# Second attention layer: the way of the turned probabilities from blocks to their places, through DRAM in place of inside SBUF

## The chip, the cores and the metric

The kernel runs on one core of one Trainium2 chip. The metric is the device time of one execution in microseconds (us), the median of several runs. The core's engines are TensorE (PE: matmuls), VectorE (DVE), ScalarE (ACT), GpSimd (POOL) and SyncE (SP). SP does no arithmetic here; it issues all transfers. Each transfer is then carried by the core's 16 DMA engines. SBUF is the on-chip memory of 128 partitions, PSUM the banks that TensorE writes, DRAM the memory outside.

## The reference, cut to what matters

Two layers, each an attention and a feed-forward, over a residual stream `x` of shape (2, 512, 512), all in float32. The change touches the second attention only:

```python
# x: (b=2, n=512, 512); H = 32 heads of HD = 128
h = layernorm(x)
q = rmsnorm((h @ Wq + bq).reshape(b, n, H, HD), gq)
k = rmsnorm((h @ Wk + bk).reshape(b, n, H, HD), gk)
v = (h @ Wv + bv).reshape(b, n, H, HD)
scores = einsum("bnhd,bmhd->bhnm", q, k) / sqrt(HD)
attn = softmax(scores, axis=-1)              # (2, 32, 512, 512)
out = einsum("bhnm,bmhd->bnhd", attn, v).reshape(b, n, H * HD)
x = x + layernorm(out @ Wo + bo)
x = x + layernorm(swiglu_ffn_with_lora(layernorm(x)))
```

## The kernel before

One function per stage runs in turn: the first attention (`grouped_attention`), a linear feed-forward, the second attention (`paired_attention`, from L660 on), then the feed-forward with the gate (`swiglu_phase`). Every fp32 product is made of three passes over a high and a low part of each operand (`product`, L83 to L85); the high part is a rounding copy by ACT, the low part a subtraction (`rest`, L90) by DVE or POOL.

**Groups, slots, tiles.** The second attention works in 8 groups of 4 heads (`NG` passes). A group has 8 slots, each one head of one of the two batches, and a slot has 4 tiles (`TB`) of 128 query rows by 512 keys. So there are 64 slots and 256 tiles. Every engine walks over the same 32 steps `n` of a group, one tile's scores per step, and at each step does what tables of numbers say is due. The tables `USES1`, `OUTS1`, `LOADS1` and `FETCH1` give the steps of the projections, the weights and the outputs; `TURN_AT, MOVE_AT, LAND_AT, PV_AT, REST_AT = 1, 4, 8, 10, 12` gives how many steps after a slot's first tile each of its parts comes. Nothing but semaphores ties the engines together, so one may be steps ahead of another. In the last group the steps run on past 32, and there the first pieces of the next stage (`Entry`) are mixed in.

**One slot.** TensorE makes a tile's scores. DVE takes the negated row maximum (L1052). ACT takes the exponential into `probs` and the row sum (L941). The product with v needs the probabilities with the keys on the partitions, so they must be transposed. DVE does this in blocks of 32 by 32 (L1067): a block is turned within its own 32 partitions and is put into `blocks`. After that, a block of query group `g` and key group `c` lies in partitions 32g to 32g+31, and its place is partitions 32c to 32c+31. The moving is done by transfers, from `blocks` to `moved`. Both tiles hold two slots, even and odd (`k = slot % 2`), of 8 KB per partition each.

**The step that is changed** is `move` on SP (L780 to L800), four steps after the slot's first tile. SP waits for the reciprocal row sums (L783) and for the last read of `inv_rows` (L785), and writes the sums to DRAM, turned, 512 elements of 4 bytes (L786). It waits for the four transposed tiles (L790) and for the product of the slot two before (L792). Then it issues 16 transfers of 32 partitions by 2 KB (L796), one per pair of g and c. Last, it reads the sums back as a broadcast into `inv_all` (L799). Each transfer raises a semaphore by 16 when it has landed; `s_move[k]` counts 16 x 16 = 256 (`MOVES`) per slot.

**Who waits.** Eight steps after the slot's first tile ACT waits for `s_move[k]` and makes the high parts `probsT_hi` (L947), two at that step and two at the next. POOL and DVE make the low parts `probsT_lo` (L90). At step 10 TensorE multiplies with v (`pv`, into `l_general`), DVE scales the result by `inv_all` (L1023), and ACT and DVE split it for the output projection (L959, L1078), whose results DVE adds to `acc` (L1085). Before DVE overwrites `blocks` it waits until the slot two before has been moved.

**What else SP has in its queue.** In order of the steps: the weights of q and k (L761, eight transfers, at steps 6 and 22), of v (L765, four, at steps 1 and 17, after a wait at L752 for TensorE to have finished with v's last projection), of the output (`raw_out`, L768, two, at steps 11 and 27, with a wait at L755), and biases (L774). In the last group there are also the residual rows and side weights of the next stage (L376, L380, at step 22), its weights (L384, L386, at step 26) and more rows (L376, at step 33). SP works through all this in order, so a wait holds up what follows.

```python
for g in range(TB):
    for c in range(TB):
        sp.dma_start(moved[32 * c:32 * c + 32, k, g],
                     blocks[32 * g:32 * g + 32, k, c]).then_inc(s_move[k], 16)
wait_past(sp, s_inv_dma, m, 32 * SLOTS, 32 * slot + 16)
sp.dma_start(inv_all[:, k], ...).then_inc(s_inv_dma, 16)
```

Of the kernel before, what the change touches and what calls it, by code (L numbers as in the profile page):

```python
# [20 lines left out]
F32 = mybir.dt.float32  # L21
F32R = mybir.dt.float32r

P = 128
B, S, D = 2, 512, 512
T = B * S
TT = T // P
TB = S // P
# [5 lines left out]
SLOTS = GH * B  # L34
# [25 lines left out]
def wait_past(engine, sem, m, per, count):  # L60

    if m.first and not (isinstance(count, int) and count > 0):
        return
    engine.wait_ge(sem, m.i * per + count)
# [176 lines left out]
class Opening:  # L241


    first, last, i = True, False, 0
# [18 lines left out]


MOVES = TB * TB * 16
TURN_AT, MOVE_AT, LAND_AT, PV_AT, REST_AT = 1, 4, 8, 10, 12


# [388 lines left out]
                self.square(act, 0, t)  # L657


def paired_attention(p, ctx0, xT, acc, ident, half, inv_rows, ahead, entry):  # L660

    nc, a = p.nc, p.a
    start = Opening()
    with ExitStack() as ctx:
# [18 lines left out]
        blocks = sb("blocks", [P, 2, TB, TB, P])  # L683
        with ExitStack() as early:
            moved = p.sb(early, "l1_moved", [P, 2, TB, TB, P])
# [57 lines left out]
        @block.sync  # L743
        def _(sp):
            def fetch(m, x, d):
                kind, r = x
                if not (m.first and d == 0 and r == 0) and m is not start:
                    was = d - (r == 0)
                    if kind == "wqk":
                        sp.wait_ge(s_bank, m.done(USES1, ("y", 1 - r, 0, 0), was))  # L750
                    elif kind == "wv":
                        sp.wait_ge(s_bank, m.done(USES1, ("v", 1 - r, 1, 1), was))  # L752
                    else:
                        sp.wait_ge(s_out, m.done(OUTS1, (1 - r, 1, TB - 1), was))
                    sp.nop(nofuse=True)  # L755
                group = m.i + d if m is not start else 0
                cols = slice(r * HW, (r + 1) * HW)
                if kind == "wqk":
                    for c in range(C):
                        for e in range(2):  # L760
                            sp.dma_start(raw_qk[:, r, c, e * HW:(e + 1) * HW],  # L761
                                         a[("l1_wq", "l1_wk")[e]][group * C + c][:, cols]).then_inc(s_raw[kind][r], 16)
                elif kind == "wv":
                    for c in range(C):
                        sp.dma_start(raw_v[:, c], a["l1_wv"][group * C + c][:, cols]).then_inc(s_raw[kind], 16)  # L765
                else:
                    for h in range(2):
                        sp.dma_start(raw_out[:, h], a["l1_wo"][group * GH + 2 * r + h]).then_inc(s_raw[kind], 16)  # L768

            def bias(m, r, d):  # L770
                group = m.i + d if m is not start else 0
                for e in range(2):
                    rows = a[("l1_bq", "l1_bk")[e]][bass.ds(group, 1)][:, r * HW:(r + 1) * HW]
                    sp.dma_start(b_qk[:, r, e * HW:(e + 1) * HW], rows.to_broadcast([P, HW])).then_inc(s_b[r], 16)  # L774

            sp.wait_ge(s_const, 32)
            sp.dma_start(b_v_all[:], a["l1_bv"]).then_inc(s_const, 16)
            sp.dma_start(acc[:, 0], a["l1_bo"].to_broadcast([P, D])).then_inc(s_const, 16)

            def move(m, slot):  # L780
                k = slot % 2
                wait_past(sp, s_inv, m, SLOTS, slot + 1)
                sp.nop(nofuse=True)  # L783
                wait_past(sp, s_inv_dma, m, 32 * SLOTS, 32 * slot)
                sp.nop(nofuse=True)  # L785
                sp.dma_start(inv_rows[k].rearrange("t p -> p t"), inv[:, TB * (slot % SLOTS):TB * (slot % SLOTS + 1)],  # L786
                             allow_slow_non_contiguous=True)\
                    .then_inc(s_inv_dma, 16)
                wait_past(sp, s_block, m, TILES, TB * (slot + 1))
                sp.nop(nofuse=True)  # L790
                if not (m.first and slot < 2):
                    sp.wait_ge(s_free, m.done(USES1, ("pv", (slot - 2) % SLOTS), -1 if slot < 2 else 0))  # L792
                    sp.nop(nofuse=True)
                for g in range(TB):
                    for c in range(TB):
                        sp.dma_start(moved[32 * c:32 * c + 32, k, g],  # L796
                                     blocks[32 * g:32 * g + 32, k, c]).then_inc(s_move[k], 16)
                wait_past(sp, s_inv_dma, m, 32 * SLOTS, 32 * slot + 16)
                sp.dma_start(inv_all[:, k], inv_rows[k].rearrange("t p -> (t p)").unsqueeze(0).to_broadcast([P, S]))\  # L799
                    .then_inc(s_inv_dma, 16)  # L800

            def body(m):
                for n in m.steps():
                    for x, d in m.turns(FETCH1, n):
                        fetch(m, x, d)
                    for x, d in m.turns(BIAS1, n):
                        bias(m, x[0], d)
                    slot = m.slot_at(n, MOVE_AT)
                    if slot is not None:
                        move(m, slot)  # L810
                    if m.last and n == Entry.ROWS_AT:
                        sp.wait_ge(s_free, m.done(USES1, ("y", 1, 1, TB - 1)))
                        entry.load_rows(sp, 0)
                        entry.load_side(sp)
                    if m.last and n == Entry.WEIGHTS_AT:
                        sp.wait_ge(s_free, m.done(USES1, ("tk", SLOTS - 1)))
                        entry.load_weights(sp)
                    if m.last and n == Entry.MORE_ROWS_AT:
                        entry.load_rows(sp, 1)

            passes(sp, body, Entry.END)

        @block.tensor
# [81 lines left out]
        def _(act):  # L905
# [37 lines left out]

            def landed_hi(m, slot, k):
                if k == 0:
                    wait_past(act, s_move[slot % 2], m, SLOTS // 2 * MOVES, (slot // 2 + 1) * MOVES)
                act.activation(probsT_hi[:, :, k], moved[:, slot % 2, :, k], ACT.Copy).then_inc(s_land_hi, 1)  # L947

            def output_hi(m, slot):
# [45 lines left out]
        def _(dve):  # L995
# [64 lines left out]
            def turn_blocks(m, n):  # L1060
                slot, t = divmod(n, TB)
                wait_past(dve, s_exp, m, TILES, n + 1)
                if t == 0 and not (m.first and slot < 2):
                    dve.nop(nofuse=True)
                    wait_past(dve, s_move[slot % 2], m, SLOTS // 2 * MOVES, slot // 2 * MOVES)
                to = blocks[:, slot % 2].rearrange("p c k x -> p k c x")[:, :, :, 32 * t:32 * t + 32]
                dve.transpose(to, probs[:, n % NPR]).then_inc(s_block, 1)  # L1067

# [1203 lines left out]
def build(nc, a, out):  # L2272
    p = Program(nc, a)
    with ExitStack() as ctx:
        ident = p.sb(ctx, "ident", [P, P])
        half = p.sb(ctx, "half", [P, TB * GH])
        acc = p.sb(ctx, "acc", [P, TT, D])
        xT, xT_words = p.split_and_words(ctx, "xT", [P, C, T])
        made = p.sem(ctx, "made")
        x_rows = a["x"].rearrange("(t p) d -> p t d", p=P)  # L2280
        out_rows = out.rearrange("(t p) d -> p t d", p=P)
        kept = nc.dram_tensor("x_kept", [T, D], F32, kind="Internal").ap().rearrange("(t p) d -> p t d", p=P)

        inv_rows = [nc.dram_tensor(f"inv_rows{layer}", [2, tiles, P], F32, kind="Internal").ap()
                    for layer, tiles in enumerate((2 * TB, TB))]

        with nc.Block() as block:
            @block.gpsimd
            def _(pool):
                pool.memset(ident[:], 0.0).then_inc(made, 1)  # L2290
                pool.wait_ge(made, 1)
                pool.affine_select(out=ident[:], in_=ident[:], compare_op=ALU.not_equal, fill=1.0, base=0,
                                   pattern=[[-1, P]], channel_multiplier=1).then_inc(made, 1)
                pool.memset(half[:], -0.5).then_inc(made, 1)
                pool.wait_ge(made, 3)

        ahead = Ahead(p, ctx, xT)
        entry = Entry(p, ctx, xT, acc, ident, half, kept)
        grouped_attention(p, ctx, xT, acc, ident, half, x_rows, kept, inv_rows[0], ahead)
        paired_attention(p, ctx, xT, acc, ident, half, inv_rows[1], ahead, entry)  # L2300
        swiglu_phase(p, ctx, xT, xT_words, acc, kept, out_rows, entry)


# [58 lines left out]
```

## Time and profile before

| what | value |
|---|---|
| median of 3 runs | 2200.83 us |
| lowest and highest run | 2198.38 and 2201.15 us |
| the profiled execution | 2198.5 us, span 2196.7 us |
| granted clock of TensorE, mean over the span | 0.984 |
| PE, DVE, ACT, POOL busy | 2089.8, 1636.8, 1348.5, 1222.3 us |
| bytes moved by DMA | 231.69 MB, mean 105 GB/s |
| second attention, from its first moves to its last product | about 854 to 1965 us |

Times within the profile are us from the start of the span. A row of the time line gives an instruction's start, its duration, its engine, its line and what it writes and reads (out<-in), then in brackets how long the engine had been idle before it and what ended this. For SP, a row is the issue of one or more transfers, not their duration. The DMA view has one digit per fortieth of its stretch, the busy share of the 16 DMA engines in tenths, with the GB/s below it; its list of issues gives KB per transfer and the median time from issue to landing, where landings could be assigned. A granted clock of 1.00 is the full level of 2.4 GHz.

### The profile page before, as it was taken

What the parts mean: (1) busy time and instruction counts of PE and PEld (TensorE: products, weight loads), DVE (VectorE), ACT (ScalarE), POOL (GpSimd) and SP (SyncE); (2) the same over time, 40 slices, a digit from 0 to 9 for tenths busy, and PEclk for the clock granted to TensorE, in tenths of its full rate; (3) what the DMA queues carried; (4) which work ended last, traced back from release to release, by engine and by line L of the source; (5) the groups of instructions that cost most, each with busy time, mean ns of one, the idle gap of its engine ahead of it and who ended that gap; (6) DMA issues with size and microseconds to landing.
All of it is one profiled execution on the core that took longest, in us unless ns stands there. A gap on an engine that the chain in (4) does not pass through costs nothing. (4 is left out here: it accounts for less than half of the span.)

```text
span 2196.7 us, 37916 instructions
## 1 busy us (share of the span) xinstructions
PE 2089.8 (95%) x10535; PEld 1757.2 (80%) x10535; DVE 1636.8 (75%) x2972; ACT 1348.5 (61%) x3637; POOL 1222.3 (56%) x985
## 2 busy tenths in 40 slices
PE   6999999999999879999999999999999999868998
PEld 4788888888888657888888888888888888756786
DVE  6778888888788776778777777777777787775422
ACT  5777777777776455656566565666656665544321
POOL 3878778787786554546454554545445463354300
PEclk9999999999999989999999999999999999979999
DMA  2644444434444513555454455444554444643210
GB/s 83 131 105 126 108 110 114 115 104 127 102 119 129 140 55 69 105 122 114 114 108 104 109 119 115 109 99 111 118 115 111 99 111 93 142 95 105 87 53 25
DMA packets 219135, 231.69 MB, mean 105 GB/s; under 512 B 100528, under 2 KB 130384, under 8 KB 218992
## 3 DMA queue, kind: packets, MB, share of 16 engines
q1 hardware_dynamic: 218992, 229.97, 43.7%
q8 instruction: 67, 1.10, 0.3%
q14 instruction: 76, 0.62, 0.2%
HBM read 114.23 MB, written 6.55 MB: 55 GB/s over the span
## 5 line engine op out<-in xcount | busy, mean ns | idle before, releaser
L90 POOL TENSOR_TENSOR l_probsT_lo<-l_moved,l_probsT_hi 128x512 fp32r<-128x512 f32 (+2 forms) x256 | 280.4, 1100 | 296.7 <-ACT l_probsT_hi L947 269.2
L941 ACT ACTIVATE l_probs<-l_score,l_negtop 128x512 f32<-128x512 f32 x256 | 175.8, 687 | 373.2 <-DVE l_negtop L1052 359.9
L90 DVE TENSOR_TENSOR l_probsT_lo<-l_moved,l_probsT_hi 128x512 fp32r<-128x512 f32 (+1 forms) x256 | 292.5, 1143 | 37.4 <-ACT l_probsT_hi L947 37.0
L1052 DVE TENSOR_REDUCE l_negtop<-l_score 128x1 f32<-128x512 f32 x256 | 175.7, 687 | 93.1 <-PE l_score L85 90.6
L1833 ACT ACTIVATE l_probs<-l_score,l_negtop 128x128 f32<-128x128 f32 (+3 forms) x256 | 134.7, 526 | 170.3 <-DVE l_negtop L1946 169.4
L83 PE MATMUL l_out<-l_w_out_lo,l_oT_hi 128*128 128x512 f32 x512 | 209.0, 408 | 6.2 <-DVE l_oT_lo L1078 4.0
L83 PE MATMUL l_score<-l_kT_lo,l_qT_hi 128*128 128x512 f32 (+3 forms) x512 | 191.0, 373 | 22.4 <-POOL l_qT_lo L90 8.9
L1946 DVE CUSTOM_DVE_ANT_0 l_score<-l_score,l_mask 128x128 f32<-128x128 f32 (+3 forms) x256 | 125.9, 492 | 106.9 <-PE l_score L85 105.5
L84 PE MATMUL l_out<-l_w_out_hi,l_oT_lo 128*128 128x512 f32 x512 | 201.7, 394 | 0.0
L85 PE MATMUL l_out<-l_w_out_hi,l_oT_hi 128*128 128x512 f32 x512 | 201.5, 393 | 0.0
L83 PE MATMUL l_general<-l_w_qk_lo,xT_hi 128*128 128x512 f32 x504 | 198.1, 393 | 2.5 <-PEq L1452 2.5
L84 PE MATMUL l_general<-l_w_qk_hi,xT_lo 128*128 128x512 f32 x504 | 198.1, 393 | 0.0
L85 PE MATMUL l_general<-l_w_qk_hi,xT_hi 128*128 128x512 f32 x504 | 197.4, 392 | 0.0
L83 PE MATMUL l_general<-l_probsT_lo,l_v_hi 128*128 128x512 f32 (+3 forms) x512 | 182.2, 356 | 14.4 <-POOL l_probsT_lo L90 9.2
L85 PE MATMUL l_general<-l_probsT_hi,l_v_hi 128*128 128x512 f32 (+3 forms) x512 | 184.9, 361 | 0.0
L84 PE MATMUL l_general<-l_probsT_hi,l_v_lo 128*128 128x512 f32 (+3 forms) x512 | 184.4, 360 | 0.0
L85 PE MATMUL l_score<-l_kT_hi,l_qT_hi 128*128 128x512 f32 (+3 forms) x512 | 184.1, 359 | 0.0
L84 PE MATMUL l_score<-l_kT_hi,l_qT_lo 128*128 128x512 f32 (+3 forms) x512 | 183.5, 358 | 0.0
L1067 DVE STREAM_TRANSPOSE l_blocks<-l_probs 128x512 f32<-128x512 f32 x256 | 177.8, 695 | 5.6 <-ACT l_probs L941 5.6
L90 POOL TENSOR_TENSOR l_w_qk_lo<-l_raw_qk,l_w_qk_hi 128x512 fp32r<-128x512 f32 x60 | 77.7, 1295 | 150.5 <-ACT l_w_qk_hi L915 150.5
L646 ACT ACTIVATE l_squares<-l_y 128x128 f32<-128x128 f32 x512 | 151.9, 300 | 11.2 <-DVE l_y L1010 11.2
L947 ACT ACTIVATE l_probsT_hi<-l_moved 128x512 fp32r<-128x512 f32 x256 | 146.9, 629 | 4.7 <-DMA l_moved<-l_blocks 4.7
(249 smaller groups left out, 6235.7 us busy)
## 6 DMA issues: line engine op xcount, KB each, us to landing
l_moved<-l_blocks SPq DMA_DIRECT2D x1024, 64.0 KB
l_moved<-l_blocks SPq DMA_DIRECT2D x512, 80.0 KB
l_inv_all<-inv_rows SPq DMA_DIRECT2D x32, 512.0 KB
l_raw_out<-l_wo SPq DMA_DIRECT2D x64, 256.0 KB, 4.3
l_inv_all<-inv_rows SPq DMA_DIRECT2D x64, 256.0 KB
l_raw_q<-l_wq SPq DMA_DIRECT2D x32, 256.0 KB, 4.0
l_raw_qk<-l_wq SPq DMA_DIRECT2D x64, 128.0 KB, 2.8
l_raw_qk<-l_wk SPq DMA_DIRECT2D x64, 128.0 KB, 2.9
```

The lines of the kernel that those rows point to most:

```text
L83: nc.tensor.matmul(out, left.hi, right.lo, start=first, stop=False, skip_group_check=True)
L84: nc.tensor.matmul(out, left.lo, right.hi, start=False, stop=False, skip_group_check=True)
L85: return nc.tensor.matmul(out, left.hi, right.hi, start=False, stop=last, skip_group_check=True)
L90: return engine.tensor_tensor(out, full, hi.bitcast(F32), ALU.subtract)
L646: last = act.activation(self.squares[:, h], self.y[:, b, t, h * HD:(h + 1) * HD], ACT.Square, accum_out=self.sumsq[:, b, j:j + 1])
L941: act.activation(probs[:, n % NPR], score[n % 2][:], ACT.Exp, bias=negtop[:, n:n + 1], accum_out=total[:, n:n + 1]).then_inc(s_exp, 1)
L947: act.activation(probsT_hi[:, :, k], moved[:, slot % 2, :, k], ACT.Copy).then_inc(s_land_hi, 1)
L1052: dve.tensor_reduce(negtop[:, n:n + 1], score[n % 2][:], AXX, ALU.max, negate=True)\
L1067: dve.transpose(to, probs[:, n % NPR]).then_inc(s_block, 1)
L1833: act.activation(probs[:, n % NPR, 0:width[t]], score[n % 2][:, 0:width[t]], ACT.Exp, bias=negtop[:, n:n + 1], scale=-1.0, accum_out=total ...
L1946: dve.tensor_tensor_reduce(out=score[n % 2][:, 0:w], in0=score[n % 2][:, 0:w], in1=mask[:, S - w:S], scale=-SCALE, scalar=3.0e38, op0=ALU. ...
```

## The change

A DRAM tensor `block_rows` is added, of two halves (even and odd slots) of 128 rows by 8 KB. `move` now ends with one store of all of a slot's `blocks` into its half, 1 MB. A new function `land`, one step later in the program, waits until this store has landed and issues four loads. Load c fills partitions 32c to 32c+31 of `moved` with the four query groups' blocks, 4 x 2 KB for each partition, 256 KB in all. The read of `inv_all` moves to the end of `land`. `s_move[k]` now counts (1 + 4) x 16 = 80 (`LANDS`) per slot, and the waits of ACT and DVE count accordingly.

```diff
+LANDS = (1 + TB) * 16
@@ move, on SP
-                for g in range(TB):
-                    for c in range(TB):
-                        sp.dma_start(moved[32 * c:32 * c + 32, k, g],
-                                     blocks[32 * g:32 * g + 32, k, c]).then_inc(s_move[k], 16)
+                sp.dma_start(block_rows[k], blocks[:, k].rearrange("p c t x -> p (c t x)")).then_inc(s_move[k], 16)
+
+            def land(m, slot):
+                k = slot % 2
+                wait_past(sp, s_move[k], m, SLOTS // 2 * LANDS, slot // 2 * LANDS + 16)
+                sp.nop(nofuse=True)
+                for c in range(TB):
+                    rows = block_rows[k].rearrange("(g i) (c x) -> c i g x", g=TB, c=TB)[c]
+                    sp.dma_start(moved[32 * c:32 * c + 32, k].rearrange("p g t x -> p g (t x)"), rows)\
+                        .then_inc(s_move[k], 16)
                 wait_past(sp, s_inv_dma, m, 32 * SLOTS, 32 * slot + 16)
                 sp.dma_start(inv_all[:, k], ...)
@@ body, on SP
                     if slot is not None:
                         move(m, slot)
+                    slot = m.slot_at(n, MOVE_AT + 1)
+                    if slot is not None:
+                        land(m, slot)
@@ landed_hi, on ACT
-                    wait_past(act, s_move[slot % 2], m, SLOTS // 2 * MOVES, (slot // 2 + 1) * MOVES)
+                    wait_past(act, s_move[slot % 2], m, SLOTS // 2 * LANDS, (slot // 2 + 1) * LANDS)
@@ turn_blocks, on DVE
-                    wait_past(dve, s_move[slot % 2], m, SLOTS // 2 * MOVES, slot // 2 * MOVES)
+                    wait_past(dve, s_move[slot % 2], m, SLOTS // 2 * LANDS, slot // 2 * LANDS)
@@ the launch
+        block_rows = nc.dram_tensor("block_rows", [2, P, TB * S], F32, kind="Internal").ap()
```

On TensorE, DVE, ACT and POOL the order of the instructions stays as it was. On SP it changes in each slot. At the layer's entry, the first slot, SP had:

```order
L765 DMA l_raw_v<-l_wv 128x256 x4
L786 DMA inv_rows<-l_inv 128x4x1
L796 DMA l_moved<-l_blocks 32x512 x16
L799 DMA l_inv_all<-inv_rows 128x512
L761 DMA l_raw_qk<-l_wq 128x256
```

and has now:

```order
L766 DMA l_raw_v<-l_wv 128x256 x4
L787 DMA inv_rows<-l_inv 128x4x1
L795 DMA block_rows<-l_blocks 128x2048
L803 DMA l_moved<-block_rows 32x4x512 x4
L806 DMA l_inv_all<-inv_rows 128x512
L762 DMA l_raw_qk<-l_wq 128x256
```

The 16 moves became one store and four loads, in the same place. At the layer's end, slots 59 to 61 of the last group, SP had:

```order
L796 DMA l_moved<-l_blocks 32x512 x16
L799 DMA l_inv_all<-inv_rows 128x512
L765 DMA l_raw_v<-l_wv 128x256 x4
L786 DMA inv_rows<-l_inv 128x4x1
L796 DMA l_moved<-l_blocks 32x512 x16
L799 DMA l_inv_all<-inv_rows 128x512
L376 DMA ffn_w_near_words<-x_kept 128x4x512
L380 DMA ffn_w_near_words<-f_a 96x512 x2
L380 DMA ffn_w_near_words<-f_b 96x512
```

and has now:

```order
L795 DMA block_rows<-l_blocks 128x2048
L766 DMA l_raw_v<-l_wv 128x256 x4
L803 DMA l_moved<-block_rows 32x4x512 x4
L806 DMA l_inv_all<-inv_rows 128x512
L787 DMA inv_rows<-l_inv 128x4x1
L795 DMA block_rows<-l_blocks 128x2048
L803 DMA l_moved<-block_rows 32x4x512 x4
L806 DMA l_inv_all<-inv_rows 128x512
L377 DMA ffn_w_near_words<-x_kept 128x4x512
L381 DMA ffn_w_near_words<-f_a 96x512 x2
L381 DMA ffn_w_near_words<-f_b 96x512
```

In every fourth slot the four transfers of v's weights come to stand between the store and the loads; all others keep their place behind `inv_all`.

## Rows read from the trace of the kernel before

**Rows 1.** The page's part 1, busy us and share of the span.

```profile
PE 2089.8 (95%) x10535; PEld 1757.2 (80%) x10535; DVE 1636.8 (75%) x2972; ACT 1348.5 (61%) x3637; POOL 1222.3 (56%) x985
```

**Rows 2.** Busy time by stretch; columns: stretch, length, PE, PEld, DVE, ACT, POOL, clock, DMA.

```profile
895.00:1886.00 991.00, 991.00 (x5243) 846.14 (x5242) 784.29 (x1183) 616.63 (x1918) 505.66 (x368) 1.00 0.50 109
```

**Rows 3.** Time line of SP, a quiet slot and the start of the next.

```profile
1405.45 0.38 SPq L786 DMA_DIRECT2D inv_rows<-l_inv  x1
1406.12 10.01 SPq L796 DMA_DIRECT2D l_moved<-l_blocks  x16
...
1422.71 10.02 SPq L796 DMA_DIRECT2D l_moved<-l_blocks  x16
```

**Rows 4.** Time lines of SP and ACT, slots 0 and 1.

```profile
853.76 12.24 SPq L796 DMA_DIRECT2D l_moved<-l_blocks  x16
...
871.91 10.02 SPq L796 DMA_DIRECT2D l_moved<-l_blocks  x16
...
867.49 1.15 ACT L947 ACTIVATE l_probsT_hi<-l_moved 128x512 fp32r<-128x512 f32 x2 [0.28 <-DMA l_moved<-l_blocks]
...
884.57 1.15 ACT L947 ACTIVATE l_probsT_hi<-l_moved 128x512 fp32r<-128x512 f32 x2 [1.56 <-DMA l_moved<-l_blocks]
```

**Rows 5.** Time line of ACT, the readings of the slots in rows 3.

```profile
1421.12 1.15 ACT L947 ACTIVATE l_probsT_hi<-l_moved 128x512 fp32r<-128x512 f32 x2
...
1440.78 1.14 ACT L947 ACTIVATE l_probsT_hi<-l_moved 128x512 fp32r<-128x512 f32 x2
```

**Rows 6.** Time lines of SP and ACT, a late slot in the steady stretch.

```profile
1649.97 15.65 SPq L796 DMA_DIRECT2D l_moved<-l_blocks  x16
...
1667.11 1.16 ACT L947 ACTIVATE l_probsT_hi<-l_moved 128x512 fp32r<-128x512 f32 x2 [1.39 <-DMA l_moved<-l_blocks]
```

**Rows 7.** Loads of 256 KB: SP's time line, then the issues' landings.

```profile
2092.41 1.75 SPq L2121 DMA_DIRECT2D xT_hi_words<-x_kept  x4
...
xT_hi_words<-x_kept SPq DMA_DIRECT2D x4, 256.0 KB, 3.2
xT_lo_words<-x_kept SPq DMA_DIRECT2D x4, 256.0 KB, 4.3
```

**Rows 8.** DMA view of 1897 to 1925 us, landings of the next stage's loads.

```profile
ffn_w_near_words<-x_kept SPq DMA_DIRECT2D x1, 1024.0 KB, 7.3
...
ffn_w_near_words<-f_b SPq DMA_DIRECT2D x1, 192.0 KB, 11.8
```

**Rows 9.** DMA view of 779 to 789 us, a store of 1 MB.

```profile
x_kept<-l_rope SPq DMA_DIRECT2D x1, 1024.0 KB, 4.4
```

**Rows 10.** DMA view of 1411 to 1412.5 us.

```profile
GB/s 0 0 328 109 164 273 164 382 109 109 55 55 0 0 0 0 0 0 0 109 109 219 55 0 0 109 0 0 109 0 0 55 0 0 0 55 55 55 109 55
...
q1 hardware_dynamic: 69, 0.11, 104.2%
```

**Rows 11.** Time line of SP, slots 61 and 62.

```profile
1902.67 0.50 SPq L380 DMA_DIRECT2D ffn_w_near_words<-f_b  x1
...
1905.63 10.30 SPq L796 DMA_DIRECT2D l_moved<-l_blocks  x16
...
1916.73 0.34 SPq L384 DMA_DIRECT2D ffn_tile_raw<-f_tile  x1
...
1920.72 1.01 SPq L768 DMA_DIRECT2D l_raw_out<-l_wo  x2
...
1922.51 12.21 SPq L796 DMA_DIRECT2D l_moved<-l_blocks  x16
```

**Rows 12.** Time line of ACT at the layer's end.

```profile
1934.02 0.63 ACT L915 ACTIVATE l_w_out_hi<-l_raw_out 128x512 fp32r<-128x512 f32 x1 [7.97 <-DMA l_raw_out<-l_wo]
...
1937.78 1.14 ACT L947 ACTIVATE l_probsT_hi<-l_moved 128x512 fp32r<-128x512 f32 x2
...
1956.77 2.17 ACT L947 ACTIVATE l_probsT_hi<-l_moved 128x512 fp32r<-128x512 f32 x4
```

**Rows 13.** Time line of DVE, the same place.

```profile
1938.95 1.35 DVE L90 TENSOR_TENSOR l_probsT_lo<-l_moved,l_probsT_hi 128x512 fp32r<-128x512 f32 x1 [0.17 <-ACT l_probsT_hi L947]
```

More of the change, by code:

```diff
@@ L657, in scalar, with paired_attention @@
                 self.square(act, 0, t)
-def paired_attention(p, ctx0, xT, acc, ident, half, inv_rows, ahead, entry):
+def paired_attention(p, ctx0, xT, acc, ident, half, inv_rows, block_rows, ahead, entry):
     nc, a = p.nc, p.a
@@ L2299, in build @@
         grouped_attention(p, ctx, xT, acc, ident, half, x_rows, kept, inv_rows[0], ahead)
-        paired_attention(p, ctx, xT, acc, ident, half, inv_rows[1], ahead, entry)
+        paired_attention(p, ctx, xT, acc, ident, half, inv_rows[1], block_rows, ahead, entry)
         swiglu_phase(p, ctx, xT, xT_words, acc, kept, out_rows, entry)
```

## The prediction

> **What bounds the kernel now.** I read the page's busy times first, then the busy times by stretch, then the queue of SP (the engine that only issues the transfers), then who waits for the moved probabilities. TensorE is busy 95% of the span [rows 1]. From 895 to 1886 us, nearly the whole second attention, it is busy 991.00 of 991.00 us at a granted clock of 1.00 [rows 2]. In that stretch nothing can be gained. Time can only be lost, and only if the moved probabilities come so late that TensorE runs dry. What is left is the entry of the layer (before 895 us) and its end (after 1886 us), where each engine waits for another.
>
> **The path of one slot.** In a quiet slot SP issues the transfer to `inv_rows` at 1405.45, the 16 moves from 1406.12 on (10.01 us, 0.63 us each) [rows 3]. How long the last move takes to land is seen where ACT waits for it: in slot 0 the moves run from 853.76 to 866.00, and ACT, idle for them, starts at 867.49, 1.5 us later [rows 4]. So a quiet slot takes 10.0 + 1.5 = **11.5 us** from its first move. ACT comes to read it at 1421.12, which is **15.0 us** after the first move; the next slot, first move 1422.71, is read at 1440.78, 18.1 us after [rows 3, 5]. So there are some 3.5 us to spare in the slots of the tighter kind. How much more is free is shown by one late slot: its moves took 15.65 us from 1649.97, ACT waited 1.39 us and read at 1667.11, 17.1 us after the first move, and TensorE lost nothing [rows 2, 6]. A slot may thus take 17 us, and I take 18 as the point at which TensorE starts to lose.
>
> **The change, part by part.** Per slot and on SP, 16 issues go and 5 come: one store of 1 MB to `block_rows`, and four loads of 256 KB back. A wait for the store stands between them. There are 64 slots. No other engine issues anything else or in another order, so all of the price is in when the probabilities land, and in what SP has queued behind its new wait.
>
> - *Issues.* An issue costs 1.75/4 = 0.44 us for this kind of load [rows 7]. The five cost 2.2 us instead of 10.0. As SP is off the bound in the steady stretch, this is worth nothing there.
> - *Loads.* Four loads of 256 KB from DRAM: issued at 2092.41, 1.75 us for four, landing in 3.2 us, and 4.3 us for the next four [rows 7]. The last starts 1.3 us after the first, so they take 1.3 + 4.3 = 5.6 us. Bounds: 1.3 + 3.2 = 4.5 below, and 7.3 above, a load of 1 MB beside other work [rows 8].
> - *Store.* Alone, a store of 1 MB from SBUF to DRAM lands in 4.4 us [rows 9]. That is the lower bound. The upper one is 11.8 us, the slowest landing that the views show in busy queues [rows 8]. Here the store follows `inv_rows`, 512 elements of 4 bytes written to DRAM. 5.5 to 7 us after the issue at 1405.45 the DMA engines stall: from 1411.0 to 1412.5 they are 104% busy over 69 packets, and in 18 of the 40 slices of that stretch nothing is moved [rows 10]. I read this as the small writes reaching memory only then, and the engines held up by them. Now the moves' issues hide it, since they last to 1416. A store issued at 1406.1 has all its data behind these writes. If it completes about when the stall ends, at 1412.5 plus 1 us, it takes **7.5 us**, and I take that value, between the bounds, since these rows come from the very place where the store will stand.
> - *Sum.* 7.5 + 0.1 for SP to go on + 5.6 = **13.2 us** against 11.5. With the bounds: 4.4 + 0.1 + 4.5 = 9.0 to 11.8 + 0.1 + 7.3 = 19.2.
>
> The Trainium skill (DMA: Bandwidth & Descriptors, section on queues, rings and completion order) says that a transfer's semaphore increment is a strongly ordered write, which lands only after every earlier write of that DMA engine, whatever its queue. By that rule the store can't be reported before the 4-byte writes are done, however short its own data are; without it the store would cost 4.4 us. No view here shows when `inv_rows` itself lands, but the stall agrees with the rule.
>
> - *Steady stretch (slots 3 to 58).* 13.2 is below 15.0 and far below 18: **0**. The cover is TensorE's own work and ACT's idle time before each exponential. In every fourth slot SP's four `wv` transfers now stand between store and loads, with their wait for TensorE (L752); those slots are of the roomy kind, and both fit in the 7.5 us in which SP waits anyway.
> - *Entry.* Slot 0: 13.7 us before, 13.2 after: 0. Slot 1: first move 871.91, ACT idle 1.56 us for it and reading at 884.57, 12.7 us after [rows 4]. Behind the eight weight transfers of 128 KB that SP issues before it (L761) the new path gives at least 13.2, and ACT and then TensorE move back by 0.5 to 1.5 us. I take **+1.0**.
> - *End.* Slot 61's first move is issued at 1905.63. Ahead of it are the residual rows, 1 MB, and side weights, of which the last, issued at 1902.67, lands 11.8 us later, 1914.5 [rows 8, 11]. The store ends no sooner. SP is then held till 1914.6, issues loads and `inv_all` (2.4 us) and comes to the weights of the feed-forward (L384, L386) at 1917.0, where it stood at 1916.73 [rows 11]; with some time for the store's own data behind all this, I take +1. `raw_out`, issued at 1920.72, kept ACT idle for 7.97 us until 1934.02, 13.3 us after its issue [rows 11, 12]. Slot 62's store is issued 1 us later than its first move was at 1922.51 [rows 11], at 1923.5, right behind `raw_out`. I give it the same 13.3 us, the nearest row, so 1936.8; with 0.1 + 5.6 its loads land at 1942.5. ACT read this slot at 1937.78 [rows 12]. It is now **4.7 us** late. DVE had been idle for it for 0.17 us [rows 13], and in DVE's order the residual sums (L1085) and the norm statistics of the next stage (L133) stand behind it. TensorE waits for the norms. So I count all 4.7. Slot 63 is read at 1956.77, 19 us after slot 62 and so with more room than in the steady stretch [rows 12]; it isn't late.
>
> Together +1.0 + 4.7 = **+5.7 us**, against the profiled execution of 2198.5 us: 2204.2. The median of the three runs shown is 2200.8, 2.3 above that execution, so the median after would be **2206.5 us**. What a measurement of this kernel can tell from no change is about 0.2%, 4.4 us: below 2196.4 is faster, above 2205.2 slower.
>
> **The rivals.**
>
> *Forecast, 0.48.* 2203 to 2212, by the value of the store in the full queues: three quarters of this is over the 0.2%.
>
> *Hidden at the end, 0.24.* If slot 62's store takes 8.5 us instead of 13.3, it lands at about the old 1937.8, and only the +1.0 at the entry stays: 2201.8; between 2199 and 2205. For it: the weights ahead of it are issued by 1920.7 and much of that will have landed by 1923.5. Against it: `raw_out` in the same place took 13.3.
>
> *Faster, 0.15, the other side.* If the small writes don't hold the store, it takes 4.4 us and the slot 4.4 + 0.1 + 5.6 = 10.1 instead of 11.5. The entry gains 1.4 us (ACT waits 1.56 there). At the end SP is free for the weights 4.4 + 0.1 + 2.4 = 6.9 us after slot 61's start instead of 10.9, `raw_out` comes up to 4 us earlier and so does the read of slot 62, of which some 3.4 would show: 2200.8 - 4.8 = 2196. It decides at a store under 5.8 us, from where the slot is shorter than 11.5. For it: the quiet store in rows 9. Against it: that one had no 4-byte writes ahead, and the stall in rows 10. In the skill, the rules for kernel authors on the same page favour it: coalesce small transfers, since under 64 KB one pays mostly overhead. By its fit of 2.0 us plus bytes over 436e3, an estimate from that page and made for another issuing path, 1 MB would take 4.4 us.
>
> *Much slower, 0.13.* If a quiet slot's path exceeds 18 us, TensorE runs dry each time. A store at 11.8 and loads at 6.9 give 18.8; 0.8 us over in 56 slots is 45 us: 2246. A milder form, with only those slots late in which SP stalls for some 3 to 5 us (15.65 instead of 10.01 in rows 6), gives 5 to 15 us over the layer: 2207 to 2222.
>
> Faster by over 0.2%: most of the faster case, 0.14. Within 0.2%: the hidden case and a quarter of the forecast's, 0.34. Slower: the rest, 0.52. The range 2194 to 2217 leaves out the worst of the much slower case and the best tenth of the faster one.
>
> **What would show it.** In the profile of the changed kernel: the store's issue and the first load's issue 7 to 8.5 us apart in quiet slots (under 6 speaks for faster, over 10 for much slower); TensorE still 100% busy from about 896 to 1887; ACT's idle time for the moved data in slots 0 and 1 at 0 to 3 us; and before slot 62 a new wait of ACT of 3 to 5 us, with all that follows shifted by that. I am wrong if the stretch from 895 to 1886 gets longer, or if slot 62 is read at the old distance from slot 61.

## The result, and the profile after

The changed kernel takes **2441.12 us** (median of 4 runs, 2437.76 to 2449.16) against 2199.61 us for the kernel before on the same chip (4 runs). The ratio is 1.1107, 95% interval 1.1073 to 1.114. The forecast of 2206.5 us had the sign right and the size wrong by 235 us; the range ended at 2217. Its profiled execution took 2437.76 us, with a span of 2436.0.

The busy times of the page after, beside [rows 1]:

```profile
PE 2170.9 (89%) x10535; PEld 1789.2 (73%) x10535; DVE 1636.0 (67%) x2972; ACT 1353.8 (56%) x3637; POOL 1208.7 (50%) x985
...
HBM read 181.34 MB, written 73.66 MB: 105 GB/s over the span
```

TensorE does the same 10535 matmuls. It is busy 81 us longer and idle 158 us longer (265.1 against 106.9). The steady stretch, busy time by stretch as in [rows 2]:

```profile
900.00:1880.00 980.00, 872.62 (x4325) 716.89 (x4323) 640.71 (x969) 511.92 (x1585) 409.22 (x306) 0.96 0.85 142
```

It was busy all of this stretch before; now it runs dry in nearly every slot (107 us in all, 2.3 per slot). Its granted clock falls from 1.00 to 0.96, and its busy time per matmul rises from 0.189 to 0.202 us. The DMA engines are busy 85% of the time in place of 50%, though they move only 142 GB/s.

**Where the time lies.** The reads of the moved probabilities on ACT's time line after, slots 0, 1, 61, 62 and 63, as in [rows 4, 12]:

```profile
872.26 1.15 ACT L957 ACTIVATE l_probsT_hi<-l_moved 128x512 fp32r<-128x512 f32 x2 [7.25 <-DMA l_moved<-block_rows]
...
892.15 1.15 ACT L957 ACTIVATE l_probsT_hi<-l_moved 128x512 fp32r<-128x512 f32 x2 [3.88 <-DMA l_moved<-block_rows]
...
2147.44 1.15 ACT L957 ACTIVATE l_probsT_hi<-l_moved 128x512 fp32r<-128x512 f32 x2 [4.61 <-DMA l_moved<-block_rows]
...
2172.30 1.15 ACT L957 ACTIVATE l_probsT_hi<-l_moved 128x512 fp32r<-128x512 f32 x2 [10.77 <-DMA l_moved<-block_rows]
...
2193.26 2.19 ACT L957 ACTIVATE l_probsT_hi<-l_moved 128x512 fp32r<-128x512 f32 x4 [1.80 <-DMA l_moved<-block_rows]
```

Before, slot 61 was read here:

```profile
1921.08 1.14 ACT L947 ACTIVATE l_probsT_hi<-l_moved 128x512 fp32r<-128x512 f32 x2
```

With slots 1, 62 and 63 of before at 884.57, 1937.78 and 1956.77 [rows 4, 12], the 239.3 us of span divide up as follows: up to slot 1 +7.6, slots 1 to 61 +218.8 (60 slots, 20.92 us each in place of 17.28), slot 61 to 62 +8.2, slot 62 to 63 +2.0, all after that +2.8.

**What SP does in a slot.** SP's time line after, two slots, beside [rows 3]:

```profile
1395.09 0.38 SPq L787 DMA_DIRECT2D inv_rows<-l_inv  x1
1395.74 0.37 SPq L795 DMA_DIRECT2D block_rows<-l_blocks  x1
1407.42 1.74 SPq L803 DMA_DIRECT2D l_moved<-block_rows  x4
1409.29 0.36 SPq L806 DMA_DIRECT2D l_inv_all<-inv_rows  x1
1415.79 0.38 SPq L787 DMA_DIRECT2D inv_rows<-l_inv  x1
1416.45 0.33 SPq L795 DMA_DIRECT2D block_rows<-l_blocks  x1
```

And what SP waits for in the layer, its waits from 900 to 2050 us (columns: engine and line, releaser, us in total, times, longest):

```profile
SPq L800 <- DMA block_rows<-l_blocks: 560.0, 55, 12.3
SPq L786 <- DMA l_inv_all<-inv_rows: 206.9, 54, 6.8
SPq L784 <- DVE l_inv L1068: 35.5, 22, 8.9
```

Two things are to be seen. The first load comes 11.68 us after the store; over slots 3 to 57 the median is 11.85. ACT reads this slot at 1415.16 after 4.09 us of idleness for it, 7.74 us after the first load. So the path is 11.68 + 7.74 = 19.4 us, where 11.5 stood before and 13.2 was forecast. And SP goes in a circle without rest: 0.65 us from `inv_rows` to the store, 11.68 to the loads, 1.87 to `inv_all`, then 6.50 until `inv_all` has landed, since the next slot's `inv_rows` waits for that (L786, at L785 before). Together 20.70 us, and TensorE's work in a slot is 17.3.

The DMA view of 1395 to 1408 us shows why the store is slow (digits: busy tenths, GB/s below):

```profile
DMA  9857599999900700000092969993323079710000
GB/s 372 315 192 52 184 403 429 353 88 25 25 0 0 25 0 0 0 0 0 0 50 25 126 50 101 50 126 25 50 50 50 25 328 403 303 51 0 0 0 0
```

A slice is 0.325 us. Up to 1398 data moves at up to 429 GB/s. Then, for some 7 us, little arrives (at most 126 GB/s in a slice, mostly 50 or less), until some 0.35 MB go in about a microsecond from 1405.4 on. I read this as the stall of [rows 10], now in front of somebody who waits.

### The profile page after: what moved, and what is told of

It reads as the page before. It is cut to its first block and busy times, and to the rows that moved or that the text cites. A ratio compares the mean times of both kernels' runs of the same rounds, so it can differ in the third digit from the quotient of the medians.

```text
span 2436.0 us, 37306 instructions
## 1 busy us (share of the span) xinstructions
PE 2170.9 (89%) x10535; PEld 1789.2 (73%) x10535; DVE 1636.0 (67%) x2972; ACT 1353.8 (56%) x3637; POOL 1208.7 (50%) x985
## 5 line engine op out<-in xcount | busy, mean ns | idle before, releaser
L83 PE MATMUL l_general<-l_probsT_lo,l_v_hi 128*128 128x512 f32 (+3 forms) x512 | 212.3, 415 | 169.8 <-DVE l_v_lo L90 106.7
L83 PEld LDWEIGHTS l_general<-l_probsT_lo,l_v_hi 128*128 128x128 f32 x512 | 108.8, 213 | 225.0 <-DVE l_v_lo L90 119.3
L84 PE MATMUL l_general<-l_probsT_hi,l_v_lo 128*128 128x512 f32 (+3 forms) x512 | 203.9, 398 | 0.0
L85 PE MATMUL l_general<-l_probsT_hi,l_v_hi 128*128 128x512 f32 (+3 forms) x512 | 203.8, 398 | 0.0
## 6 DMA issues: line engine op xcount, KB each, us to landing
block_rows<-l_blocks SPq DMA_DIRECT2D x64, 1024.0 KB, 11.9
```

The source lines that it names most:

```text
L83: nc.tensor.matmul(out, left.hi, right.lo, start=first, stop=False, skip_group_check=True)
L84: nc.tensor.matmul(out, left.lo, right.hi, start=False, stop=False, skip_group_check=True)
L85: return nc.tensor.matmul(out, left.hi, right.hi, start=False, stop=last, skip_group_check=True)
```

## The experiments

Two causes were on the table: W, the 512 small writes of `inv_rows` hold the store, and the circle on SP, where `inv_rows` waits for `inv_all`. Kernels 1 to 8 and 12 start from the changed kernel, 9 to 11 from the kernel before. "Period" below is the mean distance of the stores over slots 3 to 57 (20.92 us in the changed kernel), "store" the median landing in the DMA view or time line. Kernels 1 to 3, 5 to 7 and 12 were run once each; the differences of 70 us and more that are read from them are far above the spread of the kernel before, 2190 to 2204 us over all its runs.

**1. The store ahead of the small writes.**

```diff
+                sp.dma_start(block_rows[k], ...).then_inc(s_move[k], 16)
                 wait_past(sp, s_inv, ...); wait_past(sp, s_inv_dma, ...)
                 sp.dma_start(inv_rows[k].rearrange("t p -> p t"), ...)
-                sp.dma_start(block_rows[k], ...).then_inc(s_move[k], 16)
```

> The changed kernel with one step moved: SP issues the store of the blocks first and the transfer of the row sums to inv_rows (512 elements of 4 bytes) right behind it. In the changed kernel the store's median landing is 11.9 us and a slot takes about 21 us. Theory W (the small writes ahead of it hold the store up): the store lands in 4.5 to 6 us, the slot's period falls to the 17.4 us of the kernel before, and the time is 2195 to 2215 us. Rival S (the store is slow by itself: DRAM, or packets of 8 KB): it still takes about 12 us and the time stays above 2400 us.

Measured: 2290.80 us, period 18.57. It was expected near the time of before, so this is a miss. The stores still land in 11.9 us (median; single ones from 4.3 to 15.8). A slot of its time line:

```profile
1406.68 0.33 SPq L788 DMA_DIRECT2D block_rows<-l_blocks  x1
1408.98 0.38 SPq L793 DMA_DIRECT2D inv_rows<-l_inv  x1
1418.72 1.74 SPq L803 DMA_DIRECT2D l_moved<-block_rows  x4
```

The small writes were issued 2.3 us behind the store, and it is slow all the same. Over slots 3 to 57 they came 0.5 to 5.8 us behind (the expectation of kernel 5 says within a microsecond, which is true of 12 of these 55). How late they came matters: in the 10 slots with at most 0.75 us, 7 stores had landed after 4.4 to 5.9 us; in the other 45, from 0.9 us on, the stores took 7.9 to 15.8. Why the closest followers often do no harm isn't known. In many slots the last `inv_all` was still under way beside the store too, since the order leads to that. In slots 36 and 52 it had been issued 7.4 and 7.1 us before, and these stores took 12.8 us each; kernel 4, with this order and no writes of 4 bytes, has 4.3. The 150 us gained weren't taken apart. The path of a slot is no shorter than in the changed kernel (20.3 us against 19.7, medians), but the circle is: the wait for `inv_all` now overlaps the store.

**2. The sums as 128 pieces of 16 bytes**, in the changed kernel's order. Each partition's four sums go to neighbouring addresses, and the scaling on DVE reads them in that order.

```diff
-sp.dma_start(inv_rows[k].rearrange("t p -> p t"), inv[...])
+sp.dma_start(inv_rows[k].rearrange("t p -> (t p)").rearrange("(p t) -> p t", t=TB), inv[...])
-... tokens(inv_all[:, slot % 2]) ...
+... inv_all[:, slot % 2].rearrange("p (g i t) -> p t g i", g=TB, t=TB) ...
```

> The changed kernel with its order kept, but the row sums are written to inv_rows as 128 elements of 16 bytes instead of 512 of 4 (they lie in DRAM in another order, and VectorE reads inv_all by another stride). Theory W (small writes hold the store up, by their number): the store lands in 4.4 + 7.5/4 = 6 to 7 us, TensorE is the bound again, 2200 to 2225 us. Rival S (slow store): 12 us and over 2400 us as before. If the sums' size doesn't matter but that something stands ahead does, also about 12 us.

Measured: 2198.45 us, period 17.41. The store is quicker than the 6 to 7 us expected, so its price doesn't simply go with the number of writes. From the DMA view of its stretch 900 to 1880 us:

```profile
block_rows<-l_blocks SPq DMA_DIRECT2D x56, 1024.0 KB, 4.2
...
inv_rows<-l_inv SPq DMA_DIRECT2D x56, 2.0 KB, 2.0
```

and busy time in the same stretch:

```profile
900.00:1880.00 980.00, 979.96 (x5176) 836.25 (x5175) 791.44 (x1168) 609.75 (x1903) 492.40 (x363) 1.00 0.62 169
```

One edit that touches neither the store, the loads nor any wait takes back the whole 240 us. With stores of 4.2 us the circle takes less than TensorE's slot and is harmless.

**3. The circle cut**: other counters, and no wait for `inv_all` ahead of `inv_rows`; the small writes stay as they are. Store and row sums now share one counter, so SP waits for both before the loads.

```diff
-                wait_past(sp, s_inv_dma, m, 32 * SLOTS, 32 * slot)
-                wait_past(sp, s_move[k], m, SLOTS // 2 * LANDS, slot // 2 * LANDS + 16)
+                wait_past(sp, s_store, m, 32 * SLOTS, 32 * slot + 32)
```

> The changed kernel with its order kept and the small writes ahead of the store, but with other semaphores: store and row sums on one, the loads on one, inv_all on one, so that SP no longer waits for the last inv_all to land before it writes the next row sums (207 us of waiting in the changed kernel). The path of a slot stays at 11.9 + 7.7 = 19.6 us. Theory L (SP's serial loop of store, loads and inv_all, 21 us per slot, sets the pace): the loop shrinks to 12 + 2.2 + 1.1 = 15 us, below the 17.4 us of TensorE's work, and only the lateness of 19.6 against 18 us stays: 2205 to 2300 us. Rival M (the path's length alone sets the pace, through ACT): 2400 us or more, as in the changed kernel.

Measured: 2370.46 us, period 19.91. This lies between the ranges of both theories, so neither was right about its size. Its waits of SP and ACT, 900 to 1880 us:

```profile
SPq L798 <- DMA block_rows<-l_blocks: 576.8, 49, 14.2
```

```profile
ACT l_probsT_hi L957 <- DMA l_moved<-block_rows: 133.2, 39, 5.6
```

Without the circle 70 us of the 240 are gone, though the path of a slot has become longer: 21.1 us in the median, against 19.7, since SP's wait for store and sums together ends after 13.5. Which of the two lands last isn't shown. The other 170 us come with a path so far over 18 us. As the path of the changed kernel is shorter, the circle's share there is probably larger than 70; that wasn't measured.

**4. Both edits**: the store first and the sums packed (12 runs, 17 of the kernel before).

> Both of the first two edits: store first, row sums behind it as 128 elements of 16 bytes. Theory W: store 4.5 to 5.5 us, loads no longer held by small writes, 5.6 to 7 us, a slot's path 10 to 12 us, so about the kernel before or a little under it: 2190 to 2205 us. Rival (loads are slow for a reason of their own, 7.7 us as in the changed kernel): path 12.5 to 13.5 us, 2200 to 2210 us. Rival S: over 2400 us.

Measured: 2197.68 us against 2197.69, ratio 0.9998 (0.9988 to 1.0008). In the profiled executions the stretch from the first store or move to the read of slot 1 is 2.9 us shorter than before, and that from the read of slot 61 to the end 3.8 us longer. At the end of the layer, on SP and on ACT:

```profile
1915.93 0.84 SPq L769 DMA_DIRECT2D l_raw_out<-l_wo  x2
1916.98 0.33 SPq L788 DMA_DIRECT2D block_rows<-l_blocks  x1
```

```profile
1933.87 1.15 ACT L958 ACTIVATE l_probsT_hi<-l_moved 128x512 fp32r<-128x512 f32 x2 [5.20 <-DMA l_moved<-block_rows]
```

Slot 62's store stands right behind eight weight transfers of the feed-forward and two of `raw_out`; its loads are issued only 8.4 us later, at 1925.38, and ACT is idle for them for 5.20 us.

**5. The small writes behind the loads.** The three waits and the issue of `inv_rows` moved from `move` to `land`, between the loads and `inv_all`.

```diff
                 for c in range(TB): sp.dma_start(moved[32 * c:32 * c + 32, k]...)
+                wait_past(sp, s_inv, ...); wait_past(sp, s_inv_dma, ...)
+                sp.dma_start(inv_rows[k].rearrange("t p -> p t"), ...)
                 wait_past(sp, s_inv_dma, m, 32 * SLOTS, 32 * slot + 16)
```

> The changed kernel with the 512 small writes of the row sums issued only after the store has landed and the four loads are issued, so that they are never in flight beside a store. In e1 they were issued within a microsecond behind the store and it still took 4.3 to 15.8 us, 11.9 in the median. Theory W, widened (small writes in flight beside the store hold it up, whichever was issued first): the store lands in 4 to 5 us in every slot. SP must then wait for the sums before it reads them back, 8 to 10.5 us, so its loop is 4.5 + 2.2 + 8 to 10.5 + 1.2 = 16 to 18.4 us per slot against 17.4 us of TensorE's work: 2200 to 2260 us. Rival (e1's store was slow for another reason, such as the last slot's loads or broadcast still being under way): the store stays at 8 to 12 us and the time above 2290 us.

Measured: 2463.89 us, slower than the change itself: a miss. SP's time line:

```profile
1409.47 0.33 SPq L788 DMA_DIRECT2D block_rows<-l_blocks  x1
1417.64 1.75 SPq L796 DMA_DIRECT2D l_moved<-block_rows  x4
1419.68 0.38 SPq L802 DMA_DIRECT2D inv_rows<-l_inv  x1
1429.91 0.34 SPq L806 DMA_DIRECT2D l_inv_all<-inv_rows  x1
1430.53 0.33 SPq L788 DMA_DIRECT2D block_rows<-l_blocks  x1
```

The store is quicker (median 6.2), but SP now waits 10.2 us for the small writes before it reads them back, and the next store stands behind that wait. Two waits in series, 21.1 us again. That the store takes 6.2 and not the 4 to 5 expected wasn't traced; `inv_all` is issued 0.6 us ahead of it here. This also gives the first direct time for `inv_rows`, from its DMA view of 900 to 1880 us, behind the four loads:

```profile
inv_rows<-l_inv SPq DMA_DIRECT2D x46, 2.0 KB, 10.5
```

**6, 7 and 12. Why the small writes are slow.** To experiment 2 (packed sums) one transfer is added that nobody reads: 512 elements of 4 bytes to another DRAM tensor. The elements lie 4, 64 or 16 bytes apart; the count is the same.

```diff
+small = nc.dram_tensor("small", [2, TB, P, 1], F32)   # 6; [2, TB, P, 16] in 7, [2, TB, P, 4] in 12
+                sp.dma_start(small[k].rearrange("t p x -> p t x")[:, :, 0:1], inv[...].unsqueeze(2))
```

> The packed sums of e2 (store 4.2 us, 2198 us) and ahead of them one more transfer of the row sums into a tensor that nothing reads, 512 elements of 4 bytes side by side as in the changed kernel. Theory W: it brings the slow store back, 11 to 12 us, and 2400 to 2460 us. If e2's gain came from anything but the small writes (VectorE's other stride, the place of the sums in DRAM), the store stays at 4 to 6 us and the time at about 2200 us.

> As e6, but the 512 elements of 4 bytes go to places 64 bytes apart. Theory W1 (the number of small writes counts): as slow as e6, store 11 to 12 us, 2400 to 2460 us. Theory W2 (what costs is that neighbours of 4 bytes, written by different engines, meet in the same piece of DRAM): the store lands in 4 to 6 us and the time is about 2200 us.

> The extra transfer of 512 elements of 4 bytes that nobody reads, beside packed sums, now with its elements 16 bytes apart in DRAM (dense: 2527.6 us, stores landing in 12.7; 64 bytes apart: 2197.55 us, stores in 4.6). Theory C (the price grows with how many separate writes fall close together, here four in 64 bytes in place of sixteen, as many as the packed sums of 16 bytes have): about as quick as 64 bytes apart, 2196 to 2215 us, extra transfer landing in 2 to 4 us, stores in 4.5 to 6. Rival B (any 4-byte write whose 64 bytes are shared with another costs, whatever their number): stores in 10 to 13 us, 2400 to 2530 us.

Measured: 2527.6 us at 4 bytes (period 22.29, slower than expected), 2197.55 at 64, 2197.38 at 16 (the one run of the kernel before on that last chip took 2190.56), as theories W2 and C had it. So it is the small writes, and not the other changes that came with packing them, that make the store slow. The added transfer at 64 bytes, then at 16, with the stores beside it (DMA views, 900 to 1880 us):

```profile
block_rows<-l_blocks SPq DMA_DIRECT2D x56, 1024.0 KB, 4.6
...
small<-l_inv SPq DMA_DIRECT2D x56, 2.0 KB, 1.9
```

```profile
block_rows<-l_blocks SPq DMA_DIRECT2D x56, 1024.0 KB, 5.4
...
small<-l_inv SPq DMA_DIRECT2D x56, 2.0 KB, 2.5
```

So not the number of small writes costs, but how closely they lie: sixteen writes in 64 bytes bring the stores to 12.7 us, four in 64 bytes to 5.4, one to 4.6. Why that is so, and in which part of the chip, isn't shown; whether it matters that neighbours are carried by different DMA engines wasn't tested.

**8 to 11. What the way through DRAM is worth without its obstacle.** Kernel 8 is kernel 4 with the feed-forward's first weights (`WEIGHTS_AT`) issued at step 30 in place of 26. Kernel 9 is the kernel before with packed sums and that step, 10 with that step alone, 11 with packed sums alone.

```diff
-ROWS_AT, WEIGHTS_AT, MORE_ROWS_AT = 22, 26, 33
+ROWS_AT, WEIGHTS_AT, MORE_ROWS_AT = 22, 30, 33
```

> e4 (store first, sums packed; 2197.68 us, as the kernel before) with the next stage's weights (L384, L386) issued at step 30 instead of 26, behind the store and loads of slot 62. In e4 that slot's store, queued behind the weights, takes 8.4 us and ACT then waits 5.2 us for the slot. Theory E (the end of the layer is set by slot 62 behind the weights): the wait goes, the slot is read 4 to 5 us sooner, and the time is 3 to 5 us less, 2192.5 to 2195 us. Rival: the weights come too late for the next stage and the wait moves there: 2197 us or more.

> The kernel before (16 moves inside SBUF) with the packed sums and the weights at step 30. Here ACT waits 7.97 us for raw_out at the end, which stands behind the weights. Theory E: that wait goes too, but the moves still take 10 us of issuing: 3 to 6 us less than before, 2192 to 2195 us, so the same as e8 or within 2 us of it; then the way through DRAM is worth nothing by itself. If the way through DRAM is worth something once the small writes are gone, e8 is faster than this one by 2 us or more.

> The kernel before with one number changed: the last weights of the attention layer are issued four steps later, behind the last slot's transfers. Theory Q (the 0.2% of the last two kernels comes from the wait of 8.0 us for raw_out at the end of the layer, which this shortens or moves): 2189 to 2194 us, about 5 us below the kernel before. Rival P (the gain comes from the sums written as 16-byte pieces, which free the queue): 2196 to 2200 us, no difference. Both in part: 2194 to 2196.

> The kernel before with the sums written as 128 pieces of 16 bytes and nothing else. Theory Q (the weights' place brought the gain): 2195 to 2200 us, no difference that shows, since before the change nobody waits behind the small writes for long. Rival P: 2189 to 2194 us. In the trace inv_rows should land in about 2 us in place of about 10, and the 16 transfers inside SBUF behind it should land no later than before.

| kernel | way | packed | weights at | ratio to before, 95% interval | median |
|---|---|---|---|---|---|
| 4 | DRAM | yes | 26 | 0.9998 (0.9988 to 1.0008) | 2197.68 |
| 8 | DRAM | yes | 30 | 0.9981 (0.9969 to 0.9993) | 2192.22 |
| 9 | SBUF | yes | 30 | 0.9977 (0.9966 to 0.9988) | 2191.45 |
| 10 | SBUF | no | 30 | 0.9982 (0.9970 to 0.9995) | 2197.02 |
| 11 | SBUF | yes | 26 | **0.9961** (0.9947 to 0.9975) | 2192.06 |

Each ratio is to the kernel before on its own chip; 8 and 9 shared one, where before took 2196.62, and so did 10 and 11, where it took 2200.52. Kernel 11 beats both kernels. The wait of 7.97 us in [rows 12] is nearly gone, on SP and on ACT:

```profile
1918.59 0.85 SPq L768 DMA_DIRECT2D l_raw_out<-l_wo  x2
```

```profile
1925.21 0.63 ACT L916 ACTIVATE l_w_out_hi<-l_raw_out 128x512 fp32r<-128x512 f32 x1 [0.69 <-DMA l_raw_out<-l_wo]
```

SP reaches `raw_out` 2.1 us sooner than in [rows 11], but most of the gain is in its landing: 6.6 us from issue to ACT's start, against 13.3. Before, the writes of `inv_rows` were issued right behind it, at 1921.88; so they seem to have cost the kernel before something too.

With the same packed sums and weights at 26, the way through DRAM (4) stands at 0.9998 and the moves in SBUF (11) at 0.9961; the intervals don't meet, though they are from two chips and kernel 4 also has the store ahead of the sums. In kernel 8 slot 62 escapes the queue (store at 1919.89, loads at 1924.20), and the two ways can't be told apart (8 and 9). Nowhere is the way through DRAM worth anything. Kernels 8 and 9 came out as theory E had it, 0.3 and 0.6 us below its ranges. Theory Q failed on both kernels: packed sums were to do nothing without the change, and they do more than the weights' place (2192.06 against 2197.02 on one chip). The weights' place alone still gives a little (0.9982, clear of 1). The weights moved are those of the feed-forward, the stage behind. The two gains don't add up (9). Why not wasn't traced.

## Why the prediction was wrong

- **The view of the bound held.** Time could only be lost in the steady stretch, and only by probabilities that come late. That is what happened. The term that failed is the **0** for this stretch; between the reads of slots 1 and 61 it measured +218.8 us.
- **Store, the term that failed first.** I took 7.5 us, from the end of the stall in [rows 10], and put 11.8 only at the edge. Measured 11.85. The mechanism was the right one (the small writes), and so was the place in the trace. But I took 1.5 us in which little moved for the end of the matter. In the profile after, the stall lasts from 3 to 10 us behind the issue of `inv_rows`. Before, the moves came 0.63 us apart; as I read it, their data passing in small portions hid how long it went on. Kernel 5 gives `inv_rows` 10.5 us, behind the loads.
- **The rule on ordered writes was too narrow.** The Trainium skill (DMA: Bandwidth & Descriptors, section on queues, rings and completion order) lets a semaphore's increment land only after every earlier write of that DMA engine. No run shows whether the store is reported after the small writes: no view of the changed kernel gives their landing. And in kernel 1 the small writes are the later ones, and most stores are still slow (11.9 us in the median); the rule alone doesn't predict this.
- **Loads.** Forecast 5.6, at most 7.3; measured 7.7 from the first issue to the last landing, the 256 KB of `inv_all` right behind them included. [Rows 7] had no such company.
- **Sum.** 13.2 forecast, 19.7 measured (median). By the text's own rule, 18 us per slot, this gives (19.7 - 18) x 56 = 95 us, an estimate. That mechanism is the rival "much slower", which had 0.13; its 2246 us is still 195 us short of the measured time. The same rule comes near to kernel 3: (21.1 - 18) x 56 = 174 us, measured 172 (2370.46 - 2198.5).
- **Steady stretch, what was overlooked.** The rest is SP's circle. I counted what stands behind the new wait in program order, but only up to the end of the slot. I didn't follow it round: the next `inv_rows` waits for `inv_all` to land (L785 before), and `inv_all` had been moved behind the wait for the store. Before, SP issued `inv_all` 16 moves after `inv_rows` and had the landing covered; now 11.7 + 1.9 + 6.5 stand in a row. Kernel 3 is 70 us faster without the circle, though its path is longer. By the 18 us rule the changed kernel's path gives 95 of its 240 us and leaves some 145, an estimate; the split itself wasn't measured.
- **Entry.** Forecast +1.0, measured +7.6: slot 1 starts 1.3 us later (store at 873.20) and takes 19.0 us to its read instead of 12.7.
- **End.** Forecast +4.7, measured +8.2 for slot 62. Its loads are issued 15.8 us after the store (2148.81 to 2164.58 on SP's time line), where 13.3 was given. The 13.3 was itself a landing with small writes right behind it: in kernel 11 the same `raw_out` takes 6.6. Slot 63, which wasn't to be late, adds 2.0. The mechanism, a store behind the weights, is shown best in kernel 4, where nothing else is slow: 8.4 us behind the weights against 4.3 in kernel 8, where they come later.
- **Faster.** This rival had 0.15 and rested on a store of 4.4 us. Kernels 2 and 4 have that store, 4.2 and 4.3, and gain nothing: with the loads of the changed kernel, 4.2 + 7.7 is 11.9 against 11.5. The one slot in which ACT waits for the loads in these kernels, slot 62, has 7.9 and 8.5 us for them, so they are no quicker there. No gain shows even with the quick store.
- **The chances.** By the text's own parts, within 0.2% had 0.24 + 0.12 and slower 0.36 + 0.13; it says 0.34 and 0.52.

## What to carry to other kernels

A transfer that is hidden has no visible price: before putting a wait next to it, measure how long it takes with somebody waiting, and don't read it off the part of it that shows. When a wait is added on the engine that issues transfers, follow its loop over a whole iteration, to the next time it issues the same thing, and compare the sum of the waits in that loop with the bounding engine's work per iteration. A transposed write of a small vector to DRAM as single 4-byte elements side by side is to be suspected first: store it in whatever order gives each partition one run, and undo the order where it is read.

## What the runs showed of the hardware

- 512 writes of 4 bytes, side by side in DRAM, take 10.5 us to land behind 1 MB of loads (kernel 5), and they hold a store in flight: 1 MB takes 11.9 us beside them (the changed kernel) and 4.2 with packed sums (kernel 2). 512 such writes 16 bytes apart land in 2.5 us (kernel 12), 64 bytes apart in 1.9 (kernel 7), and 128 writes of 16 bytes, side by side, in 2.0 (kernel 2).
- A store issued ahead of the small writes isn't safe from them: 11.9 us in the median (kernel 1). It was mostly quick, 4.4 to 5.9 us, only where they came at most 0.75 us behind it.
- In part of the stall the DMA engines count as busy: 0.85 at 142 GB/s in the changed kernel, against 0.62 at 169 in kernel 2. It isn't a sure sign. Kernel 1, with stores just as slow, has 0.64 at 160.
- 1 MB from SBUF to DRAM and back into other partitions takes some 11.9 us without the small writes, put together from the store of kernel 2 (4.2) and the loads of the changed kernel (7.7). 16 moves of 64 KB inside SBUF take 11.5, 10.0 of it the time to issue them.
